# A mixture-of-experts kernel on one core: weight remainders by accumulating DMA, and half 0's way into block 2 a step sooner

## The chip, the cores and the metric

The kernel runs on one core of a Trainium2 chip. The metric is the device time of one execution in microseconds; lower is better. TensorE multiplies, VectorE (DVE), ScalarE (ACT) and GpSimd (POOL) work on arrays, and SyncE (SP) issues transfers. Each engine runs its own instruction stream in order, and semaphores tie the streams together.

## The reference, cut to what matters

Two residual blocks work on 1024 tokens of width 256, in float32. The first picks one of four experts by token id and gates with silu(g) * u where the up and gate weights are the same array; the second picks two of eight experts by a learned router.

```python
x = x + xattn(layernorm(x), token_ids, ctx, ctx, ctx)
#   for e in range(4): y = (silu(h @ W[e].T) * (h @ W[e].T)) @ W[e].T, kept where expert_ids == e
x = x + ffn(layernorm(x), Wg, W1, W2, W3)
#   scores = h @ Wg.T; the best 2 of 8, softmax of their scores as weights w
#   for e in range(8): y += w[e] * (silu(h @ W1[e].T) * (h @ W2[e].T)) @ W3[e].T   (176 hidden units)
```

## The kernel before

Every float32 product is made of three products of rounded operands: an operand is split into a rounded part `hi` (a copy to fp32r) and the remainder `lo` (operand minus `hi`), and hi*hi, hi*lo and lo*hi are summed in PSUM. This holds for the weights (`w_hi`, `w_lo`), the normalised and transposed tokens (`hT_hi`, `hT_lo`) and the activations (`act_hi`, `act_lo`).

The tokens are cut into two halves of 512 columns. The hidden units of all experts together are cut into chunks of 128: 8 in block 1 and 11 in block 2. A step is one chunk of one half in one block, and the 38 steps run in the order block, half, chunk: steps 0 to 7 and 8 to 15 are block 1, 16 to 26 and 27 to 37 are block 2. `up(q)` (L669) writes the step's hidden units into PSUM banks `z` with 6 matmuls of 512 columns in block 1 and 12 in block 2; `down(q)` (L700) adds their product with the down weights into `y[h]` with 12 matmuls of 256 columns. `LAG` is 3: TensorE does `up(q)`, the stages of slot 0, `down(q - 3)`, then the stages of slot 1 (L746 to L759).

Between the two, ScalarE takes silu from PSUM (L416). In block 1 GpSimd multiplies it by the gate (`gated`, L337) and VectorE by the up product (`act`, L587); in block 2 VectorE does both (L577, L587). ScalarE rounds `act` (`round_act`, L388), VectorE takes the remainder (`act_low`, L552). The buffers of these are three deep.

Weights come in 19 pieces, one for each chunk of each block: 8 of 128 x 512 float32 (256 KB) and 11 of 128 x 768 (384 KB). SyncE loads them into a ring of five raw slots (`load_piece`, L249); a slot is loaded again once the remainder of the piece in it is taken (L253). ScalarE makes `w_hi` from a raw piece (`weight_hi`, L350), and the remainder `w_lo` is a subtract on VectorE for the pieces of `VECTOR_LO` ((0,0), (0,5), (0,6), (0,7), L558) and on GpSimd for the other fifteen (L289). `SPLIT_AT` says at which step a piece is split: (0,4) and (0,5) at step 1, (0,6) at 2, (0,7) at 3, then (1,0) at 6, (1,1) at 8, (1,2) at 10, (1,3) at 14 (its subtract on GpSimd a step later, `LATE_LO`), and (1,c) at 12 + c from c = 4 on. `up(q)` waits for the remainder of its piece (`wait_lo`, L671).

Three ways lead tokens into a (block, half) other than the first: into (0,1), (1,0) and (1,1). `STAGES` (L77) gives for each way at what step, counted from `WAY_START` (0, 8 and 16), each engine does its part; for TensorE there is a slot too. A way into block 2 is: the sum of the residual (`add_block`, L501, VectorE), statistics (L460), the power of the variance on GpSimd (L299) and the shift (L306), normalisation of two tiles by VectorE (L485) and two by ScalarE (L371), eight token transposes (L641), `tokens_hi` (L362, ScalarE), `tokens_lo` (L492, VectorE), the router's scores (L653, L657), a copy of them (L433), four score transposes (L665), `best_two` (L507, VectorE), the tanh (L437, ScalarE), the softmax and its gate rows (L527, VectorE), four gate transposes (L627) and the copy `gates_out` (L380, ScalarE). The engines work these in program order within their step: at a step ScalarE does silu, `tokens_hi`, `round_act` of the step before, the score copy, tanh, gates, then the pieces and normalisations due. The first up products of block 2 need `act` of earlier steps: `up(16)` needs act(13) and `up(17)` needs act(15) (L677), since the banks are paired differently; later ones need silu and gated of two steps before (L680). At step 10 VectorE also makes the router's remainder (L594).

## Time and profile before

| | |
|---|---|
| median of 3 runs | 164.11 us (164.03 to 164.11) |
| the profiled execution | 164.04 us |
| its span in the trace | 162.2 us |
| TensorE matmuls busy | 154.5 us, 95% of the span, 904 matmuls |
| VectorE busy | 111.7 us, 69% |
| ScalarE busy | 67.8 us, 42% |
| GpSimd busy | 57.2 us, 35% |
| granted TensorE clock | 0.999 |

The span is the time from the first to the last record of the core; 1.84 us of the execution lie around it. Matmul records overlap, because matmuls are pipelined: one of 512 columns is shown with 0.39 us where the next starts 0.23 us later. So TensorE's pace is read from the starts and not from the durations, and a standstill is a start that comes later than this pace allows. What stands in brackets behind a row of a timeline is the idle time before it and what ended it. The rows are shown below, after the change.

### The profile page before, as it was taken

The page shows a single profiled execution, that of the slowest core. Times are in us where ns is not written, and L with a number is a line of the kernel's source. Part 1 is how long each engine was busy: PE and PEld are TensorE (multiplying, and loading weights), DVE is VectorE, ACT ScalarE, POOL GpSimd, SP SyncE. Part 2 cuts the span into 40 slices and gives each one's busy share as a digit, 9 for nine tenths or more (in the row PEclk, how much of TensorE's full clock was granted, in tenths as well). Part 3 has the DMA queues.
Part 4 walks back from the last instruction along what each step waited for, and adds up shares of the span by engine and source line. Part 5 has one row for each costly group of instructions (what it writes and reads, how often), then busy time and mean ns, then how long its engine had stood idle before and what let it go on. Part 6 is the DMA issues. An engine that isn't in the chain of part 4 may idle for free.

```text
span 162.2 us, 2463 instructions
## 1 busy us (share of the span) xinstructions
PE 154.5 (95%) x904; PEld 131.0 (81%) x904; DVE 111.7 (69%) x224; ACT 67.8 (42%) x121; POOL 57.2 (35%) x50
## 2 busy tenths in 40 slices
PE   7999899899999999999999799999999999999991
PEld 2477698789897788888889488888888888888890
DVE  0878999785986756799999947917444744444453
ACT  3385775754618622474335812324222222222210
POOL 0679956469767480555467310000000000000000
PEclk9999999999999999999999999999999999999999
DMA  3976353032030003033000000000000300000003
GB/s 107 349 246 191 82 203 107 0 97 76 29 97 0 2 0 101 0 97 97 0 4 0 0 0 2 4 0 0 0 0 4 129 0 0 0 2 4 0 0 129
DMA packets 4620, 8.76 MB, mean 54 GB/s; under 512 B 768, under 2 KB 1408, under 8 KB 4608
## 3 DMA queue, kind: packets, MB, share of 16 engines
q1 hardware_dynamic: 4176, 8.34, 16.3%
q10 hardware_dynamic: 432, 0.27, 0.5%
q8 instruction: 7, 0.11, 0.3%
q14 instruction: 5, 0.04, 0.1%
HBM read 7.55 MB, written 1.05 MB: 53 GB/s over the span
## 4 chain that ended last, share of the span: by engine, by line
PE 65%; DVE 21%; issue 4%; ACT 4%; POOL 3%; DVEq 0%; ACTq 0%; POOLq 0%
PE z L685 36%; PE y L710 22%; DVE act L587 5%; PE z L720 4%; DVE act_lo L552 4%; DVE norm L485 2%; DVE w_lo L558 2%; POOL gated L337 2%; DVE stats L468 2%; DVE hT_lo L492 1%; ACT act_hi L388 1%; ACT silu L416 1%; POOL rstd L299 1%; PE y L627 1%; DVE x_sb L498 1%
## 5 line engine op out<-in xcount | busy, mean ns | idle before, releaser
L685 PE MATMUL z<-hT_hi,w_hi 128*128 128x512 f32 x120 | 47.4, 395 | 1.1 <-ACT hT_hi L362 0.9
L685 PE MATMUL z<-hT_hi,w_lo 128*128 128x512 f32 x120 | 47.1, 393 | 0.0
L710 PE MATMUL y<-w_hi,act_lo 128*128 128x256 f32 x152 | 43.5, 286 | 1.0 <-DVE act_lo L552 0.9
L552 DVE TENSOR_TENSOR act_lo<-act,act_hi 128x512 fp32r<-128x512 f32 x38 | 33.6, 884 | 14.8 <-ACT act_hi L388 14.5
L710 PE MATMUL y<-w_hi,act_hi 128*128 128x256 f32 x152 | 43.0, 283 | 0.0
L710 PE MATMUL y<-w_lo,act_hi 128*128 128x256 f32 x152 | 42.9, 283 | 0.0
L416 ACT ACTIVATE silu<-z 128x512 f32<-128x512 f32 x38 | 22.6, 595 | 41.1 <-PE z L685 41.1
L685 PE MATMUL z<-hT_lo,w_hi 128*128 128x512 f32 x120 | 37.3, 392 | 0.0
L289 POOL TENSOR_TENSOR w_lo<-raw,w_hi 128x768 fp32r<-128x768 f32 (+1 forms) x15 | 27.5, 1845 | 20.3 <-ACT w_hi L353 18.9
L388 ACT CAST act_hi<-act 128x512 fp32r<-128x512 f32 x38 | 23.4, 617 | 19.7 <-DVE act L587 19.4
L710 PEld LDWEIGHTS y<-w_hi,act_lo 128*128 128x128 f32 x152 | 29.0, 191 | 3.2 <-DVE act_lo L552 1.5
L577 DVE TENSOR_TENSOR gated<-gate,z 128x512 f32<-128x512 f32 x22 | 15.0, 683 | 22.2 <-PE z L685 20.2
L710 PEld LDWEIGHTS y<-w_lo,act_hi 128*128 128x128 f32 x152 | 29.0, 191 | 1.1
L710 PEld LDWEIGHTS y<-w_hi,act_hi 128*128 128x128 f32 x152 | 29.0, 191 | 0.0
L685 PEld LDWEIGHTS z<-hT_hi,w_hi 128*128 128x128 f32 x120 | 22.7, 189 | 5.3 <-issue 1.6
L685 PEld LDWEIGHTS z<-hT_lo,w_hi 128*128 128x128 f32 x120 | 22.5, 188 | 5.4 <-DVE hT_lo L492 0.5
L685 PEld LDWEIGHTS z<-hT_hi,w_lo 128*128 128x128 f32 x120 | 22.7, 189 | 3.5
L337 POOL TENSOR_TENSOR gated<-silu,gate 128x512 f32<-128x512 f32 x16 | 22.8, 1437 | 7.1 <-ACT silu L416 7.1
L587 DVE TENSOR_TENSOR act<-gated,silu 128x512 f32<-128x512 f32 x22 | 20.0, 908 | 0.0
L353 ACT CAST w_hi<-raw 128x768 fp32r<-128x768 f32 (+1 forms) x19 | 13.9, 743 | 4.1 <-DMA raw<-weights_dram 4.1
L587 DVE TENSOR_TENSOR act<-gated,z 128x512 f32<-128x512 f32 x16 | 10.9, 679 | 1.2 <-POOL gated L337 1.2
L720 PE MATMUL z<-warm_sb 128*128 128x512 bf16 x24 | 7.2, 473 | 1.2 <-DVE warm_sb L561 1.2
(52 smaller groups left out, 80.8 us busy)
## 6 DMA issues: line engine op xcount, KB each, us to landing
raw<-weights_dram SPq DMA_DIRECT2D x11, 384.0 KB, 3.1
raw<-weights_dram SPq DMA_DIRECT2D x8, 256.0 KB, 4.5
x_sb<-x_dram SPq DMA_DIRECT2D x4, 256.0 KB, 4.4
out_dram<-x_sb SPq DMA_DIRECT2D x2, 256.0 KB, 2.5
out_dram<-x_sb SPq DMA_DIRECT2D x2, 128.0 KB, 2.0
out_dram<-x_sb ACTq DMA_DIRECT2D x2, 128.0 KB, 2.1
consts_sb<-consts_dram SPq DMA_DIRECT2D x1, 68.0 KB, 3.7
ids_sb<-token_ids_dram ACTq DMA_DIRECT2D x1, 4.0 KB, 3.9
```

The lines of the kernel that those rows point to most:

```text
L289: nc.gpsimd.tensor_tensor(w_lo[b][:, c, :], raw_piece(b, c), w_hi[b][:, c, :].bitcast(F32), ALU.subtract).then_inc(w_lo_pool, 1)
L337: nc.gpsimd.tensor_tensor(gated[:, q % BUFFERS, :], silu[:, q % BUFFERS, :], gate[:, h, :], ALU.mult)\
L353: nc.scalar.copy(w_hi[b][:, c, :], raw_piece(b, c)).then_inc(w_hi_done, 1)
L388: nc.scalar.copy(act_hi[:, q % BUFFERS, :], act[:, q % BUFFERS, :]).then_inc(act_hi_done, 1)
L416: nc.scalar.activation(silu[:, q % BUFFERS, :], z_banks(q)[0][:], ACT.Silu).then_inc(silu_done, 1)
L468: last = nc.vector.bn_stats(stats[:, t, :], src[:, t, :])
L552: nc.vector.tensor_tensor(act_lo[:, i, :], act[:, i, :], act_hi[:, i, :].bitcast(F32), ALU.subtract)\
L577: nc.vector.tensor_tensor(gated[:, i, :], gate[:, h, :], z_banks(q)[1][:], ALU.mult)\
L587: nc.vector.tensor_tensor(act[:, i, :], gated[:, i, :], factor, ALU.mult).then_inc(act_done, 1)
L685: return nc.tensor.matmul(bank[:], w[b][:, c, cols], tokens[:, h, k, :], **flags)
L710: last = nc.tensor.matmul(o, a[:, q % BUFFERS, rows], w[b][:, c, wd], start=(first and j == 0), stop=(c == CHUNKS[b] - 1 and j == 2), skip ...
L720: nc.tensor.matmul(z[3][:], warm_sb[:, 0:P], warm_sb[:], start=True, stop=True)
```

## The change

Fourteen of the 19 remainders, those of (0,5), (0,6), (0,7) and of all pieces of block 2, are made in another way: ScalarE writes the negated rounded piece into `w_lo` (an activation Copy with scale -1 into fp32r), and then GpSimd issues a DMA that reads the weights from DRAM a second time and adds them onto `w_lo`. `up(q)` waits for that DMA. SyncE may load the raw slot again once the negation is done. VectorE keeps the remainder of (0,0), GpSimd those of (0,1) to (0,4). The late subtract of (1,3) is gone: the DMA is issued at the step of its split. VectorE's three and GpSimd's eleven subtracts are gone; ScalarE has fourteen negations more, each behind the piece's cast, and GpSimd fourteen issues.

Half 0's way into block 2 is one step sooner from the token transposes on (all stages from there to the copy of the gates); its sum, statistics and normalisation stay. The scores of half 1 move at step 23 from slot 0 to slot 1, behind that step's down product.

```diff
-    "transpose_tokens": ((7, 0), (6, 0), (6, 1)),
-    "tokens_hi": (7, 5, 6),
-    "tokens_lo": (6, 4, 6),
-    "scores": (None, (7, 0), (7, 0)),
-    "score_rows": (None, 7, 7),
-    "transpose_scores": (None, (8, 0), (8, 0)),
-    "best_two": (None, 7, 8),
-    "tanh": (None, 7, 8),
-    "softmax": (None, 7, 8),
-    "transpose_gates": ((3, 0), (9, 0), (10, 1)),
-    "gates_out": (2, 8, 9),
+    "transpose_tokens": ((7, 0), (5, 0), (6, 1)),
+    "tokens_hi": (7, 4, 6),
+    "tokens_lo": (6, 3, 6),
+    "scores": (None, (6, 0), (7, 1)),
+    "score_rows": (None, 6, 7),
+    "transpose_scores": (None, (7, 0), (8, 0)),
+    "best_two": (None, 6, 8),
+    "tanh": (None, 6, 8),
+    "softmax": (None, 6, 8),
+    "transpose_gates": ((3, 0), (8, 0), (10, 1)),
+    "gates_out": (2, 7, 9),
...
-VECTOR_LO = ((0, 0), (0, 5), (0, 6), (0, 7))
-LATE_LO = (1, 3)
+VECTOR_LO = ((0, 0),)
+POOL_LO = ((0, 1), (0, 2), (0, 3), (0, 4))
+def by_dma(b, c):
+    return (b, c) not in VECTOR_LO + POOL_LO
...
         def wait_lo(engine, b, c):
-            vector = [p for p in VECTOR_LO if p <= (b, c)]
             if (b, c) in VECTOR_LO:
-                engine.wait_ge(w_lo_vector, len(vector))
+                engine.wait_ge(w_lo_vector, VECTOR_LO.index((b, c)) + 1)
+            elif (b, c) in POOL_LO:
+                engine.wait_ge(w_lo_pool, POOL_LO.index((b, c)) + 1)
             else:
-                engine.wait_ge(w_lo_pool, piece_no(b, c) - len(vector))
+                engine.wait_ge(w_lo_in[b][c], 16)
...
-                    wait_lo(sp, *((0, n) if n < CHUNKS[0] else (1, n - CHUNKS[0])))
+                    last = (0, n) if n < CHUNKS[0] else (1, n - CHUNKS[0])
+                    if by_dma(*last):
+                        sp.wait_ge(w_negated, negated_no(*last))
+                    else:
+                        wait_lo(sp, *last)
...
+            def add_weights(b, c):
+                pool.wait_ge(w_negated, negated_no(b, c))
+                nc.gpsimd.dma_start(w_lo[b][:, c, :], (weights1, weights2)[b][:, c, :], accum_op=ALU.add)\
+                    .then_inc(w_lo_in[b][c], 16)
...
-                if LATE_LO in SPLIT_AT.get(q - 1, ()):
-                    weight_lo(*LATE_LO)
                 for piece in SPLIT_AT.get(q, ()):
-                    if piece not in VECTOR_LO and piece != LATE_LO:
+                    if by_dma(*piece):
+                        add_weights(*piece)
+                    elif piece in POOL_LO:
                         weight_lo(*piece)
...
                 nc.scalar.copy(w_hi[b][:, c, :], raw_piece(b, c)).then_inc(w_hi_done, 1)
+                if by_dma(b, c):
+                    nc.scalar.activation(w_lo[b][:, c, :], raw_piece(b, c), ACT.Copy, scale=-1.0).then_inc(w_negated, 1)
```

## Rows read from the trace of the kernel before

**Rows 1.** The chain of waits in order of time: start us, us, what.
```profile
70.96 2.75 PE z L685 x12
73.71 1.43 PE y L710 x12
```

**Rows 2.** Timeline of TensorE: start us, us, engine, line, operation, tiles, [idle before, releaser].
```profile
19.00 0.63 PE L685 MATMUL z<-hT_lo,w_hi 128*128 128x512 f32 x2
20.22 0.38 PE L710 MATMUL y<-w_hi,act_lo 128*128 128x256 f32 x1 [0.59 <-DVE act_lo L552]
...
30.98 0.28 PE L710 MATMUL y<-w_hi,act_hi 128*128 128x256 f32 x1
31.85 0.47 PE L685 MATMUL z<-hT_hi,w_hi 128*128 128x512 f32 x1 [0.59 <-ACT hT_hi L362]
...
50.33 1.04 PE L641 MATMUL y<-consts_sb,norm 128*128 128x128 f32 x8
51.64 0.39 PE L710 MATMUL y<-w_hi,act_lo 128*128 128x256 f32 x1 [0.27 <-DVE act_lo L552]
...
66.12 0.28 PE L710 MATMUL y<-w_hi,act_hi 128*128 128x256 f32 x1
66.54 0.47 PE L685 MATMUL z<-hT_hi,w_hi 128*128 128x512 f32 x1
...
90.68 0.61 PE L685 MATMUL z<-hT_lo,w_hi 128*128 128x512 f32 x2
92.33 0.62 PE L653 MATMUL y<-hT_hi,router_hl 128*16 128x512 f32 x2 [1.03 <-DVE hT_lo L492]
```

**Rows 3.** Timeline of VectorE, steps 1 to 3, 9 to 11 and 15.
```profile
16.79 1.68 DVE L558 TENSOR_TENSOR w_lo<-raw,w_hi 128x512 fp32r<-128x512 f32 x1
18.39 1.78 DVE L552 TENSOR_TENSOR act_lo<-act,act_hi 128x512 fp32r<-128x512 f32 x1
...
21.79 0.68 DVE L552 TENSOR_TENSOR act_lo<-act,act_hi 128x512 fp32r<-128x512 f32 x1
...
40.70 1.28 DVE L498 TENSOR_TENSOR x_sb<-y,x_sb 128x512 f32<-128x512 f32 x2
...
43.09 1.23 DVE L594 TENSOR_TENSOR router_hl<-router_raw,router_hl 128x16 fp32r<-128x16 f32 x1
44.25 1.39 DVE L468 BATCH_NORM_STATS2 stats<-x_sb 128x6 f32<-128x256 f32 x4
...
46.17 0.16 DVE L476 TENSOR_SCALAR var<-mv 128x4 f32<-128x4 f32 x1
...
60.21 0.19 DVE L512 COPY score_part<-y 128x32 f32<-128x32 f32 x1 [1.22 <-PE y L665]
...
63.09 0.63 DVE L541 COPY gate_rows<-w_tok 128x128 f32<-128x128 f32 x4
```

**Rows 4.** Timeline of ScalarE, steps 1 to 2 and 11.
```profile
15.45 1.14 ACT L353 CAST w_hi<-raw 128x512 fp32r<-128x512 f32 x2
16.50 0.59 ACT L416 ACTIVATE silu<-z 128x512 f32<-128x512 f32 x1
...
48.11 1.09 ACT L371 ACTIVATE norm<-x_sb,shift,rstd 128x256 f32<-128x256 f32 x2 [4.27 <-POOL shift L306]
```

**Rows 5.** Timeline of GpSimd, steps 1 and 11.
```profile
15.38 1.01 POOL L299 TENSOR_TENSOR rstd<-var,minus_half 128x4 f32<-128x4 f32 x1
...
16.62 1.30 POOL L289 TENSOR_TENSOR w_lo<-raw,w_hi 128x512 fp32r<-128x512 f32 x1
...
46.41 1.39 POOL L299 TENSOR_TENSOR rstd<-var,minus_half 128x4 f32<-128x4 f32 x1 [0.86 <-DVE var L476]
```

**Rows 6.** SyncE's timeline, and busy tenths of DMA and issues, 18.6 to 21.5.
```profile
17.94 0.33 SPq L254 DMA_DIRECT2D raw<-weights_dram  x1
...
DMA  0000949413631687999999999998999989999693
...
raw<-weights_dram SPq DMA_DIRECT2D x1, 384.0 KB, 3.5
```

More of the change, by code:

```diff
@@ L187, in ffn_moe @@
         w_in = [[sem(f"w_in{b}_{c}") for c in range(CHUNKS[b])] for b in range(2)]
+        w_lo_in = [[sem(f"w_lo_in{b}_{c}") if by_dma(b, c) else None for c in range(CHUNKS[b])] for b in range(2)]
         w_hi_done, w_lo_pool, w_lo_vector = sem("w_hi_done"), sem("w_lo_pool"), sem("w_lo_vector")
+        w_negated = sem("w_negated")
         router_hi_done, router_lo_done = sem("router_hi_done"), sem("router_lo_done")
@@ L213, in wait_lo, with negated_no @@
         def wait_lo(engine, b, c):
-            vector = [p for p in VECTOR_LO if p <= (b, c)]
             if (b, c) in VECTOR_LO:
-                engine.wait_ge(w_lo_vector, len(vector))
-            else:
-                engine.wait_ge(w_lo_pool, piece_no(b, c) - len(vector))
+                engine.wait_ge(w_lo_vector, VECTOR_LO.index((b, c)) + 1)
+            elif (b, c) in POOL_LO:
+                engine.wait_ge(w_lo_pool, POOL_LO.index((b, c)) + 1)
+            else:
+                engine.wait_ge(w_lo_in[b][c], 16)
+        def negated_no(b, c):
+            return piece_no(b, c) - len(VECTOR_LO) - len(POOL_LO)
         def raw_piece(b, c):
@@ L324, in _ @@
             for c in range(FIRST_PIECES):
-                if (0, c) not in VECTOR_LO:
+                if (0, c) in POOL_LO:
                     weight_lo(0, c)
```

## The prediction

> **What bounds the kernel now.** I read the chain of waits first. From 57 us on it is TensorE nearly without a break: a step of block 2 is 2.75 us of twelve up matmuls and 1.43 us of twelve down matmuls [rows 1]. That is 0.229 us for an up matmul and 0.119 us for a down matmul, so a step of block 1, with six up matmuls, is 1.37 + 1.43 = 2.80 us; nothing in the diff removes or shortens one. So only TensorE's standstills can be won or added. I then read TensorE's timeline for starts that come later than these pitches allow [rows 2]; five of them lie where the diff reaches:
> - before the down product of step 1, 19.00 + 2 x 0.229 = 19.46 against 20.22: 0.76 us, and its first matmul is 0.10 us slower than the pitch. It waits for VectorE's act_lo.
> - before step 8's up product, 30.98 + 0.12 = 31.10 against 31.85: 0.75 us, and 0.16 us in its first matmuls. It waits for ScalarE's hT_hi.
> - after half 0's token transposes (the eight take 1.04 us, of which the next matmul can overlap some 0.14, so 50.33 + 0.90 = 51.23 against 51.64): 0.41 + 0.11 us, act_lo again.
> - before step 18's up product, 66.24 against 66.54: 0.30 + 0.08 us. The gates of half 0 (step 17's transposes) come too late.
> - before half 1's scores, 90.68 + 0.46 = 91.14 against 92.33: 1.19 us, hT_lo.
>
> Sum 0.86 + 0.91 + 0.52 + 0.38 + 1.19 = 3.86 us. That is all that this change can win, whatever it does to the load of the other engines. A shorter busy time of GpSimd or VectorE in block 2 is worth nothing by itself.
>
> **The remainders of pieces (0,5) to (0,7).** VectorE loses three subtracts; the first took 1.68 us at 16.79 and stood ahead of act_lo(1), which then took 1.78 us instead of its free 0.68 us [rows 3]; GpSimd was in its gating pass then. ScalarE gets a negation each, put at its cast's pace, half of 1.14 us [rows 4]. Then act_lo(1) ends near 18.9: ScalarE's two casts end at 16.6, the negation at 17.1, silu(2) and act_hi(1) at some 0.55 us each (the spacing of 0.59 us passes) at 18.2 [rows 4], and act_lo(1) adds 0.68. The down product could start at 19.46, and the 0.86 us go.
>
> What is late next is the new wait. `up(5)` now needs a transfer that has no counterpart in this trace. On GpSimd's queue it stands behind the subtract of piece (0,4), 16.62 + 1.30 = 17.92 [rows 5]; the negation (17.1) is done by then. GpSimd's time to issue it: at least SP's 0.33 us an issue, at most about the 1.39 us that a tiny power takes there [rows 5, 6]. I take 1.0, since both are work done in software rather than an array pass. Data: two plain loads of 384 KB are issued from 17.94 on, and with both in flight the second took 3.5 us; the 16 engines are full from 19.8 to 21.4 [rows 6]. The accumulating 256 KB comes on top. So the landing is bounded by 17.92 + 0.33 + 2.5 = 20.75 (two thirds of that load's 3.5 us) and by 17.92 + 1.39 + twice 3.5 = 26.3 (if reading and adding doubles it). I take 17.92 + 1.0 + 3.5 = 22.4: the load in the same crowd is the nearest row. `up(5)` would otherwise start at 19.46 + 1.43 = 20.9. New standstill: 1.5 + 0.1 us. Queued behind the transfer on GpSimd is gated(2), 18.9 to 20.2 (1.30 us, as the subtract of the same size [rows 5]); act(2) then ends near 20.9, and its down product is due only at 23.8. The transfers of (0,6) and (0,7) are issued behind gated(2) and gated(3), at 20.2 and 22.5, so they would land at 24.7 and 27.0; they are needed at 25.2 and 28.1. They are covered, by 0.5 and 1.1 us.
>
> The Trainium skill (DMA: Bandwidth & Descriptors, Anatomy of one DMA) has a fixed 2.0 us plus bytes over 436 GB/s for a transfer issued from GpSimd. That would be 2.6 us for 256 KB, landing at 20.5, with no standstill at `up(5)`; it is an estimate from the page for a lone plain transfer, and it is what the rival "hidden" below would look like.
>
> **Piece (1,0) and `up(8)`.** `up(4)` ended at 19.46, so it began near 18.0. Without the stall of `up(5)` TensorE's walk 18.0 + 4 x 2.80 + 0.9 + 0.1 gives 30.2 for `up(8)`; with it 31.8. ScalarE now has at step 6 a negation behind the cast of (1,0), half as long again as one of block 1 (768 columns for 512), some 0.8 us, ahead of silu(7) and hT_hi. The other engines' walk: GpSimd has issued (0,7) by 23.5, ScalarE's two normalisations (1.09 us [rows 4]) hold silu(5) to 25.3, gated(5) ends at 26.6, act(5) behind act_lo(4) at 27.4; then ScalarE's act_hi(5) 28.0, cast 28.8, negation 29.5, silu(7) 30.1, hT_hi 30.7. So hT_hi hides behind the down product as long as TensorE is the later one. The 0.91 us go, `up(8)` starts at 31.8, and to there nothing is won: 1.77 us removed, 1.6 added.
>
> **Half 0 one step sooner.** Count from F, the end of the down product of step 7. TensorE reaches the token transposes of step 13 at F + 3 x 1.37 + 2 x 1.43 = F + 7.0 and would end them at F + 7.9. The tokens: sum 1.28, act_lo and act 1.2, the router's remainder (1.23 as measured beside a GpSimd pass, a tenth or two free), statistics 44.25 to 46.33 = 2.08 [rows 3], the power 1.0 to 1.4 and the shift 0.2 (from 16.39 to the subtract's start at 16.62) [rows 5], ScalarE's two normalisations 1.09 [rows 4], and 0.2 for five handovers: F + 7.3 to F + 8.5, and the last 0.55 us of transposes after that. The standstill is between 0 and 1.1 us. I take 0.8 + 0.1, since gated(11) falls on the router's remainder as the subtract did before. It is new, and the 0.52 us behind these transposes goes (the scores of step 14 now stand before that down product).
>
> **Gates of half 0.** From the scores' copy to the last gate row VectorE needs 60.21 to 63.72 = 3.5 us [rows 3]. From the score transposes (step 15) to the gate transposes (step 16, first slot) TensorE has 1.43 + 2.75 = 4.2 us of work. It fits, and the 0.38 us go. But ScalarE now waits for the tanh at step 14, before the cast of (1,3), its negation (0.75 us each) and silu(15); GpSimd has the issue of (1,3) ahead of gated(15). From the copy of the scores: tanh +1.9, cast and negation +3.4, silu +4.0, issue of 1.0 us done by then +4.4, gated(15) 1.3, act(15) 0.7: +6.4. `up(17)` needs act(15) and is due at 4.2 + 0.45 + 1.43 = +6.1. New standstill 0.3 + 0.1 us (none if GpSimd issues in 0.33 us, 0.7 if in 1.4).
>
> **Scores of half 1 behind the down product.** 1.43 us of ready work goes in front of a wait of 1.19 us. It goes wholly; the score copy on ScalarE has the next up product (2.75 us) as cover. VectorE's and ScalarE's passes ahead of hT_lo also get shorter or stay.
>
> **Block 2's other pieces.** (1,4) to (1,10): ScalarE gets 0.74 us a step. Its step is then silu 0.6, act_hi 0.5, cast and negation 1.5, with 1.1 us of normalisations or hT_hi at two steps: 3.7 of 4.18 us. Each transfer has three steps, over 12 us, before its up product. Cost nothing. Loads are released by the negation, earlier or equal.
>
> **The sum.** Removed 3.86; added 1.6 (`up(5)`) + 0.9 (transposes) + 0.4 (`up(17)`) = 2.9. Net -0.96 us: 164.04 - 0.96 = 163.1 us for the profiled run, which is 0.07 under the median 164.11. I predict 163.1.
>
> **Rivals.**
> - Hidden: the transfer lands before 20.9. Then `up(5)` costs nothing, but ScalarE's walk (30.7 against 30.2) becomes the bound at `up(8)` and gives 0.7 back. 163.1 - 1.6 + 0.7 = 162.2. For: loads alone land near 3 us. Against: full DMA engines from 19.8 on [rows 6].
> - The transfer is slow: every 1 us beyond 22.4 is 1 us at `up(5)`. It is slower than before from a landing at 23.4 on; at 24.5 the time is 165.2. For: it reads two places and follows two loads. Against: it is only 256 KB. Later pieces ride behind the same delay, so it is paid once.
> - The earlier way backfires: transposes wait 1.1 and act(15) comes 1 us later than said, because ScalarE and GpSimd wait in turn. 163.1 + 0.3 + 0.9 = 164.3, no change.
> - The change doesn't lighten what it says: GpSimd's issues block it as long as the subtracts (1.3 to 1.8 us). Then issue times above run to the upper ends: 163.1 + 0.4 + 0.3 = 163.8.
>
> **How the numbers follow.** My forecast (162.6 to 163.7) 0.42, hidden (161.6 to 162.6) 0.20, slow transfer 0.20, backfire 0.10, issue as long as subtract 0.08. Some 0.2% (0.33 us) is about what a measurement can tell from no change: faster is below 163.8, slower above 164.4. Faster: 0.42 + 0.20 and a little of the last: 0.63. Same: most of the backfire, half of the last: 0.15. Slower: 0.22. The range leaves out the fast end of "hidden" and the slow end of "slow transfer": 161.8 to 165.2.
>
> **What would show it.** Right: TensorE waits at its fifth up product for a DMA by 1 to 2 us, and the down product of step 1 starts by 19.5; no wait before `up(8)`, before step 18 and before half 1's scores; a wait of 0.5 to 1 us inside the token transposes of step 13; VectorE's passes in block 2 at 0.68 us without the ones over 2 us. Wrong: a landing outside 21.5 to 23.4, waits for (0,6) or (0,7), issues above 1.4 us on GpSimd, or a wait of more than 1 us at `up(17)`.

## The result and the profile after

The changed kernel took 166.91, 167.39 and 168.79 us in three executions (median 167.39), the kernel before 164.11 us beside it (median of four): a ratio of 1.0202, 95% interval [1.0168, 1.0236]. A fourth execution, at 391.25 us, was disturbed and is left out. The change makes the kernel slower, by some 2%, where I had forecast 163.1 us. The profiled execution is the one of 166.91 us, with a span of 165.1 us, 2.9 us more than before.

From the page of the changed kernel (busy us, share of the span, instructions; then DMA queues; then issues with KB each and median us to landing):

```profile
PE 154.5 (94%) x904; PEld 131.2 (79%) x904; DVE 101.9 (62%) x221; ACT 77.4 (47%) x135; POOL 45.6 (28%) x53
...
q0 software_dynamic: 2016, 5.11, 18.8%
q1 hardware_dynamic: 4176, 8.34, 16.2%
...
raw<-weights_dram SPq DMA_DIRECT2D x11, 384.0 KB, 3.6
w_lo<-weights_dram POOLq DMA_DIRECT2D x11, 384.0 KB, 5.4
...
w_lo<-weights_dram POOLq DMA_DIRECT2D x3, 256.0 KB, 6.2
```

TensorE's work is the same 154.5 us. VectorE has 9.8 us less and GpSimd 11.6 us less, ScalarE 9.6 us more. The load did move as intended; the time went the other way. So I repeat the reading of before: where does TensorE stand still? Its timeline after (start us, us, engine, line, operation, tiles, [idle before, releaser]), where lines of `up` are L710 and those of `down` L735:

```profile
19.14 0.62 PE L710 MATMUL z<-hT_lo,w_hi 128*128 128x512 f32 x2
20.97 0.39 PE L735 MATMUL y<-w_hi,act_lo 128*128 128x256 f32 x1 [1.20 <-DVE act_lo L577]
...
22.39 0.28 PE L735 MATMUL y<-w_hi,act_hi 128*128 128x256 f32 x1
24.19 0.50 PE L710 MATMUL z<-hT_hi,w_hi 128*128 128x512 f32 x1 [1.52 <-DMA w_lo<-weights_dram]
...
26.99 0.28 PE L735 MATMUL y<-w_hi,act_hi 128*128 128x256 f32 x1
27.41 0.50 PE L710 MATMUL z<-hT_hi,w_hi 128*128 128x512 f32 x1
...
49.06 0.62 PE L710 MATMUL z<-hT_lo,w_hi 128*128 128x512 f32 x2
50.82 1.55 PE L666 MATMUL y<-consts_sb,norm 128*128 128x128 f32 x8 [1.15 <-DVE norm L510]
52.13 0.36 PE L735 MATMUL y<-w_hi,act_lo 128*128 128x256 f32 x1
...
65.24 0.28 PE L735 MATMUL y<-w_hi,act_hi 128*128 128x256 f32 x1
66.59 0.47 PE L710 MATMUL z<-hT_hi,w_hi 128*128 128x512 f32 x1 [1.07 <-DVE act L612]
```

Taken with the same pitches as [rows 2] (0.229 us for an up matmul, 0.119 for a down matmul), with the slow first matmul behind each gap:

| standstill | before | predicted | after |
|---|---|---|---|
| down product of step 1 (act_lo(1)) | 0.86 | 0 | 1.47 |
| `up(5)` (remainder of (0,5)) | 0 | 1.6 | 1.79 |
| `up(6)` (remainder of (0,6)) | 0 | 0 | 0.40 |
| `up(8)` (hT_hi) | 0.91 | 0 | 0 |
| in and behind half 0's token transposes | 0.52 | 0.9 | 1.79 |
| `up(18)` before, `up(17)` after | 0.38 | 0.4 | 1.30 |
| half 1's scores | 1.19 | 0 | 0 |
| sum | 3.86 | 2.9 | 6.75 |

The sum rises by 2.9 us, and so does the span. Nothing else is needed to account for the profiled run.

The two engines around the first standstill, VectorE's and GpSimd's timelines after:

```profile
16.74 1.29 POOL L306 TENSOR_TENSOR w_lo<-raw,w_hi 128x512 fp32r<-128x512 f32 x1
...
17.98 1.06 POOL L312 DMA_DIRECT2D w_lo<-weights_dram  x1
...
18.26 2.65 DVE L577 TENSOR_TENSOR act_lo<-act,act_hi 128x512 fp32r<-128x512 f32 x1 [1.27 <-ACT act_hi L413]
...
18.80 1.55 POOL L360 TENSOR_TENSOR gated<-silu,gate 128x512 f32<-128x512 f32 x1
...
20.07 1.14 POOL L312 DMA_DIRECT2D w_lo<-weights_dram  x1
...
20.69 1.86 POOL L360 TENSOR_TENSOR gated<-silu,gate 128x512 f32<-128x512 f32 x1
```

VectorE starts act_lo(1) at 18.26, even earlier than the 18.39 of before [rows 3], since its subtract of (0,5) is gone. But it takes 2.65 us where it had taken 1.78 and needs 0.68: it ends 0.56 us behind gated(2), and gated(2) itself comes later, behind the issue.

### The profile page after: what moved, and what is told of

It is laid out like the page before. It is cut to its first block, busy times and chain, and to the rows that moved or that the text cites. A ratio compares the mean times of both kernels' runs of the same rounds, so it can differ in the third digit from the quotient of the medians.

```text
span 165.1 us, 2477 instructions
## 1 busy us (share of the span) xinstructions
PE 154.5 (94%) x904; PEld 131.2 (79%) x904; DVE 101.9 (62%) x221; ACT 77.4 (47%) x135; POOL 45.6 (28%) x53
## 3 DMA queue, kind: packets, MB, share of 16 engines
q0 software_dynamic: 2016, 5.11, 18.8%
## 4 chain that ended last, share of the span: by engine, by line
PE 71%; DVE 8%; POOL 8%; DMA 7%; issue 2%; ACT 2%; DVEq 0%; ACTq 0%; POOLq 0%
PE z L710 41%; PE y L735 27%; DMA w_lo<-weights_dram 4%; POOL w_lo L306 3%; DMA x_sb<-x_dram 2%; POOL gated L360 2%; POOL rstd L322 2%; DVE stats L493 2%; PE y L666 2%; DVE act_lo L577 1%; DVE router_hl L619 1%; DVE act L612 1%; DVE x_sb L643 1%; POOL w_lo L312 1%; PE y L678 1%
## 5 line engine op out<-in xcount | busy, mean ns | idle before, releaser
L710 PE MATMUL z<-hT_hi,w_hi 128*128 128x512 f32 x120 | 47.6, 397 | 3.1 <-DMA w_lo<-weights_dram 1.5
L710 PE MATMUL z<-hT_hi,w_lo 128*128 128x512 f32 x120 | 47.1, 393 | 0.0
L735 PE MATMUL y<-w_hi,act_lo 128*128 128x256 f32 x152 | 43.5, 286 | 1.7 <-DVE act_lo L577 1.7
L735 PE MATMUL y<-w_lo,act_hi 128*128 128x256 f32 x152 | 43.0, 283 | 0.0
L735 PE MATMUL y<-w_hi,act_hi 128*128 128x256 f32 x152 | 43.0, 283 | 0.0
L710 PE MATMUL z<-hT_lo,w_hi 128*128 128x512 f32 x120 | 37.2, 391 | 0.0
L735 PEld LDWEIGHTS y<-w_hi,act_lo 128*128 128x128 f32 x152 | 29.0, 191 | 3.7 <-DVE act_lo L577 1.6
L735 PEld LDWEIGHTS y<-w_lo,act_hi 128*128 128x128 f32 x152 | 29.0, 191 | 1.1
L735 PEld LDWEIGHTS y<-w_hi,act_hi 128*128 128x128 f32 x152 | 29.0, 191 | 0.0
L710 PEld LDWEIGHTS z<-hT_hi,w_hi 128*128 128x128 f32 x120 | 22.7, 189 | 7.7 <-DMA w_lo<-weights_dram 2.1
L413 ACT CAST act_hi<-act 128x512 fp32r<-128x512 f32 x38 | 23.4, 616 | 8.4 <-DVE act L612 8.3
L710 PEld LDWEIGHTS z<-hT_lo,w_hi 128*128 128x128 f32 x120 | 22.5, 188 | 5.2 <-DVE hT_lo L517 0.3
L710 PEld LDWEIGHTS z<-hT_hi,w_lo 128*128 128x128 f32 x120 | 22.7, 189 | 3.6
L312 POOL DMA_DIRECT2D w_lo<-weights_dram x14 | 12.8, 912 | 31.8 <-ACT w_lo L378 31.8
L612 DVE TENSOR_TENSOR act<-gated,silu 128x512 f32<-128x512 f32 x22 | 15.1, 684 | 0.0
L378 ACT ACTIVATE w_lo<-raw 128x768 fp32r<-128x768 f32 (+1 forms) x14 | 11.2, 799 | 0.0
```

Of the source, the lines that this page charges most:

```text
L312: nc.gpsimd.dma_start(w_lo[b][:, c, :], (weights1, weights2)[b][:, c, :], accum_op=ALU.add)\
L378: nc.scalar.activation(w_lo[b][:, c, :], raw_piece(b, c), ACT.Copy, scale=-1.0).then_inc(w_negated, 1)
L413: nc.scalar.copy(act_hi[:, q % BUFFERS, :], act[:, q % BUFFERS, :]).then_inc(act_hi_done, 1)
L612: nc.vector.tensor_tensor(act[:, i, :], gated[:, i, :], factor, ALU.mult).then_inc(act_done, 1)
L710: return nc.tensor.matmul(bank[:], w[b][:, c, cols], tokens[:, h, k, :], **flags)
L735: last = nc.tensor.matmul(o, a[:, q % BUFFERS, rows], w[b][:, c, wd], start=(first and j == 0), stop=(c == CHUNKS[b] - 1 and j == 2), skip ...
```

## The experiments

The first four undo or isolate one part each. What an experiment is compared with is the kernel before, measured beside it (164.1 to 164.4 us); its diff is against the kernel that its text names.

**The remainders by DMA alone.**

```diff
 STAGES = {                # the table of the kernel before, everything else as changed
-    "transpose_tokens": ((7, 0), (5, 0), (6, 1)),
+    "transpose_tokens": ((7, 0), (6, 0), (6, 1)),
...
```

> The changed kernel with the old order of the stages: only the fourteen remainders by DMA. In the changed kernel's trace the standstills at act_lo(1), up(5) and up(6) sum to 3.7 us and replace 1.8 us (before the down product of step 1 and before step 8). Theory A (the remainders carry the loss): some 2 us slower than before, so 166.0. Theory B (the stages moved sooner carry it): within 0.3 us of before, 164.1.

Measured: 166.37 us, ratio 1.0104 [1.0069, 1.0140]. Theory A holds. Its ten times fall in two groups, four of 164.99 to 165.22 and six of 166.3 to 166.98. The mean granted clock of TensorE is 0.996 to 1.0 in the first group and 0.985 to 0.99 in the second. That scatter, which the kernel before doesn't have, became a question of its own.

**The moved stages alone.**

```diff
 STAGES = {                # the table of the changed kernel, everything else as before
-    "transpose_tokens": ((7, 0), (6, 0), (6, 1)),
+    "transpose_tokens": ((7, 0), (5, 0), (6, 1)),
...
```

> The kernel before with all stages moved as in the change, remainders as before. It wins 1.2 us at half 1's scores. At half 0 it trades 0.9 us of standstills (before the down product of step 11, before step 18) for a wait in the token transposes of step 13 and one before up(17). Theory A: those two new waits come from the stages' own chain (statistics, power, tanh ahead of silu(15)) and are as long as in the changed kernel, 1.8 and 1.3 us: 164.1 - 1.2 - 0.9 + 3.1 = 165.1. Theory C: the negation and the issue ahead of silu(15) and gated(15) make the second wait; without them it is nearly gone: 163.8.

Measured: 165.48 us, ratio 1.0070 [1.0052, 1.0087]. The token transposes wait 1.35 us (I had expected 1.8) and `up(17)` 1.37 us, without any DMA remainder. Theory A holds and C falls: the negation and the issue aren't needed for the second wait. So half 0's earlier way loses as it stands, and hides the gain at half 1's scores.

**Half 1's scores alone.**

```diff
-    "scores": (None, (7, 0), (7, 0)),
+    "scores": (None, (7, 0), (7, 1)),
```

> The kernel before with only half 1's scores moved behind the down product of step 23. Every theory: the standstill of 1.19 us goes and nothing replaces it, 164.1 - 1.2 = 162.9.

Measured: 163.01 us, ratio 0.9917 [0.9890, 0.9944]. As expected; this part alone beats the kernel before.

**Block 1's remainders back on VectorE.**

```diff
-VECTOR_LO = ((0, 0),)
+VECTOR_LO = ((0, 0), (0, 5), (0, 6), (0, 7))     # all else as in the changed kernel
```

> The changed kernel with the remainders of (0,5), (0,6), (0,7) on VectorE again; all eleven of block 2 stay with the DMA. Theory A (the loss sits in block 1's three transfers, their landing of over 6 us and GpSimd's issue holding act_lo back): the standstills to step 8 fall from 3.7 us to the 1.8 us of before or less, so about 2 us under the changed kernel, 165.2. Rival (the transfers of block 2 hurt too, by the memory or the port): it stays above 166.5.

Measured: 164.68 us, ratio 1.0007 [0.9990, 1.0024]. The loss by DMA sits in block 1's three transfers. A new thing showed: `up(8)` waits 1.49 us for hT_hi. ScalarE's timeline of this run:

```profile
29.90 0.62 ACT L413 CAST act_hi<-act 128x512 fp32r<-128x512 f32 x1 [2.62 <-DVE act L612]
30.42 0.83 ACT L376 CAST w_hi<-raw 128x768 fp32r<-128x768 f32 x1
...
31.16 0.84 ACT L378 ACTIVATE w_lo<-raw 128x768 fp32r<-128x768 f32 x1
31.91 0.57 ACT L441 ACTIVATE silu<-z 128x512 f32<-128x512 f32 x1
...
32.38 1.06 ACT L387 CAST hT_hi<-y 128x512 fp32r<-128x512 f32 x2
```

The negation of (1,0) (0.75 us to the next pass) stands ahead of hT_hi as the prediction said. It costs its full length here, 1.49 us of waiting against 0.75 before. In the changed kernel it costs nothing, only because TensorE is late there.

**The moved stages, repaired in two places.**

```diff
-ROUTER_STEP = 10
+ROUTER_STEP = 7           # in the kernel of the moved stages alone
```

> The stages moved as in the change, remainders as before, and the router's remainder at step 7 instead of 10, off the chain between half 0's sum and its statistics. Its pass took 1.23 us there (beside GpSimd's subtract). Theory A (that chain sets the wait in the token transposes of step 13): the wait falls from 1.35 us by up to 1.2 us, and the time by about as much against the stages alone, 165.5 to 164.4. Rival (the wait hangs on the power on GpSimd or on ScalarE): it stays at 1.3 us and so does the time.

Measured: 164.54 us, ratio 1.0017 [0.9998, 1.0035]: 0.9 us under the stages alone. The wait in and behind the transposes fell from 1.35 to 0.68 us in the profile. A pass of 1.23 us on 16 columns [rows 3], which takes 0.67 us where no GpSimd pass lies beside it, was on the chain.

```diff
 ROUTER_STEP = 7
-SPLIT_AT |= {q: ((1, c),) for c, q in enumerate((6, 8, 10, 14))}
+SPLIT_AT |= {q: ((1, c),) for c, q in enumerate((6, 8, 10, 15))}
```

> The same, and piece (1,3) is split at step 15 (its subtract at 16) instead of 14. Theory A (up(17) waits since the cast of (1,3) stands ahead of silu(15) and its subtract on GpSimd holds act_lo(14) and so act(15)): the 1.37 us before up(17) go, and with the scores' 1.2 us the kernel reaches about 162.6, under the kernel with the scores alone. Rival (act(15) is late because of the tanh and nothing else): the wait shrinks by the cast's 0.7 us at most, 163.7.

Measured: 163.09 us, ratio 0.9916 [0.9886, 0.9946], and no wait at `up(17)` is left. VectorE and GpSimd around act(15), first with the split at 14 (the stages alone), then at 15:

```profile
60.28 1.29 POOL L337 TENSOR_TENSOR gated<-silu,gate 128x512 f32<-128x512 f32 x1 [4.94 <-ACT silu L416]
...
61.53 1.85 POOL L289 TENSOR_TENSOR w_lo<-raw,w_hi 128x768 fp32r<-128x768 f32 x1
61.58 2.35 DVE L552 TENSOR_TENSOR act_lo<-act,act_hi 128x512 fp32r<-128x512 f32 x1
...
63.85 0.67 DVE L587 TENSOR_TENSOR act<-gated,z 128x512 f32<-128x512 f32 x1
```

```profile
59.05 1.30 POOL L337 TENSOR_TENSOR gated<-silu,gate 128x512 f32<-128x512 f32 x1 [4.21 <-ACT silu L416]
60.98 0.69 DVE L552 TENSOR_TENSOR act_lo<-act,act_hi 128x512 fp32r<-128x512 f32 x1
...
61.58 0.68 DVE L587 TENSOR_TENSOR act<-gated,z 128x512 f32<-128x512 f32 x1
```

The subtract that began 0.05 us before act_lo(14) held it for its whole length, and act(15) stands behind act_lo(14). The edit also takes the cast of (1,3) from ahead of silu(15), so gated(15) comes sooner as well; the two shares aren't separated. The rival (the tanh alone) would have left a wait. But 163.09 us is no better than the scores alone: repaired, half 0's earlier way is about worth what the later one was.

**What makes the landing late: the addition or the crowd.**

```diff
-                nc.gpsimd.dma_start(w_lo[b][:, c, :], (weights1, weights2)[b][:, c, :], accum_op=ALU.add)\
+                nc.gpsimd.dma_start(w_lo[b][:, c, :], (weights1, weights2)[b][:, c, :])\
```

The rest is the changed kernel.

> The changed kernel with the fourteen transfers as plain ones from GpSimd, without the addition (w_lo is then overwritten with the weights instead of becoming the remainder; the addition is left out). Landings in the changed kernel: 4.7 to 7.3 us from the start of the issue, 6.2 for (0,5). Theory D (adding onto the destination makes the transfers slow): landings fall to about an issue of 0.9 us plus the 3.1 to 3.6 us of plain loads, 4.0 to 4.5, and up(5) waits at most 0.3 us; 1.5 us or more under the changed kernel. Theory E (the way through GpSimd or the crowd of loads makes them slow): landings stay at 5 to 7 us and up(5) waits 1.5 us.

Measured: 164.92 us, ratio 1.0038 [1.0015, 1.0061]. All fourteen landings went from 4.7 / 5.9 / 7.3 us (least, median, most, from the start of the issue) to 3.2 / 4.1 / 5.4, that of (0,5) from 6.2 to 4.7, and `up(5)` waited 0.51 us. The addition costs a transfer 1.5 to 1.9 us; of this the issue on GpSimd is some 0.3 us (0.53 to 0.78 us plain, 0.86 to 1.14 with the addition). The same 2016 packets and 5.11 MB took 10.3% of the DMA engines' span plain and 18.8% with the addition. Theory D is right on the direction but not all of it: `up(5)` still waited. And not all of the gain is at `up(5)`. With the shorter issues act_lo(1) took 2.46 us instead of 2.65, and the wait before `up(17)` was 0.92 us instead of 1.23.

The other half of the question, in the kernel with the remainders by DMA alone:

```diff
             def load_piece(b, c):
+                if (b, c) == (1, 1):
+                    for k in (5, 6, 7):
+                        sp.wait_ge(w_lo_in[0][k], 16)
```

> The kernel with the remainders by DMA and the old stages; SyncE holds the plain loads of (1,1) and later back until (0,5), (0,6), (0,7) have landed. Theory I (the crowd of two 384 KB loads makes (0,5) land 6.2 us after the start of its issue): it lands after 4.3 to 4.8 us like the fastest of block 2, so near 22.5; up(5) waits some 0.2 us instead of 1.8, as act_lo(1) still holds the down product to 20.9. About 1.5 us under the 166.4: 164.9. Rival (the addition alone takes the 6 us): it lands at 24 as before, 166.4.

Measured: 163.75, 163.78, 166.70 and 166.82 us. In the profiled execution (163.78 us) (0,5) landed 4.1 us after the start of its issue with the addition still in it, where the same kernel without this edit has 6.3, and `up(5)` doesn't wait. So the crowd of two plain loads of 384 KB costs some 2 us. Both theories hold, one half each; no run takes both away at once. The issues of (0,5) as the three kernels' DMA views list them (the changed kernel; plain; loads later):

```profile
w_lo<-weights_dram POOLq DMA_DIRECT2D x1, 256.0 KB, 6.2
```

```profile
w_lo<-weights_dram POOLq DMA_DIRECT2D x1, 256.0 KB, 4.7
```

```profile
w_lo<-weights_dram POOLq DMA_DIRECT2D x1, 256.0 KB, 4.1
```

**What holds act_lo(1).** First, does GpSimd's issue itself hold a pass of VectorE that reads two arrays in SBUF? The changed kernel gets plain transfers more:

```diff
+                if 29 <= q < 34:
+                    pool.wait_ge(gated_done, q + 1)
+                    for k in range(3):
+                        nc.gpsimd.dma_start(raw[:, q - 29, k * D:(k + 1) * D], weights2[:, q - 29, k * D:(k + 1) * D])...
```

> The changed kernel with 15 plain transfers of 128 KB more, issued by GpSimd three by three in steps 29 to 33, behind VectorE's gated, so that they lie beside act_lo and act, both of which read two arrays in SBUF; nothing else runs on GpSimd there. Theory P (GpSimd's issue holds VectorE's two-array passes as its array passes do): those of the passes that begin inside an issue take 1.0 to 3 us instead of 0.68. Theory Q (only GpSimd's array passes hold them; in the changed kernel it was gated behind the issue): all stay at 0.68 to 0.70 us.

```profile
125.36 1.66 POOL L374 DMA_DIRECT2D raw<-weights_dram  x3 [27.46 <-DVE gated L609]
125.51 0.69 DVE L584 TENSOR_TENSOR act_lo<-act,act_hi 128x512 fp32r<-128x512 f32 x1 [0.45 <-ACT act_hi L420]
126.11 0.68 DVE L619 TENSOR_TENSOR act<-gated,silu 128x512 f32<-128x512 f32 x1
```

No: both passes lie inside the issues and keep 0.68 us, in the other steps too. Theory Q. The same execution (168.69 us) happened to show act_lo(1) at 4.95 us:

```profile
18.43 4.95 DVE L584 TENSOR_TENSOR act_lo<-act,act_hi 128x512 fp32r<-128x512 f32 x1 [1.27 <-ACT act_hi L420]
...
19.10 1.55 POOL L361 TENSOR_TENSOR gated<-silu,gate 128x512 f32<-128x512 f32 x1
...
20.96 1.86 POOL L361 TENSOR_TENSOR gated<-silu,gate 128x512 f32<-128x512 f32 x1
```

It ends 0.56 us behind gated(3): it waited for gated(2), and then for gated(3) too. TensorE stood still for 3.57 us ahead of that down product, and then ran at the lower of its two clock levels, 1.2 GHz, for 3.4 us (stretch, length, busy us of each engine, granted clock, share and rate of the DMA engines):

```profile
23.40:26.80 3.40, 3.36 (x14) 3.27 (x15) 1.97 (x4) 2.79 (x6) 0.82 (x2) 0.50 0.89 221
```

So the price of such an execution has three parts: 2.2 us more of waiting at act_lo(1) (3.57 against 1.37), some 1.4 us by the clock (the down product and `up(5)` took 4.43 us together instead of 3.0), and 1.8 us back, since `up(5)` no longer has to wait for (0,5). The sum, 1.8 us, is an estimate from these rows; this execution took 1.8 us more than the profiled one of the changed kernel. The mean granted clock is 0.99 here, as in the execution of 168.79 us of the changed kernel.

Then, does an accumulating issue hold it? In the kernel with the remainders by DMA alone:

```diff
                     if by_dma(*piece):
+                        if b == 1:
+                            pool.wait_ge(gated_done, q + 1)
                         add_weights(*piece)
```

> The same kernel, the transfers of (1,4) to (1,10) issued only once VectorE's gated of the step is done, so that an accumulating issue of 0.88 us of 384 KB stands beside act_lo or act, which read two arrays in SBUF. The 128 KB plain issues left these at 0.69 us. Theory G (an accumulating issue is no different): 0.68 to 0.70 us again, and act_lo(1)'s first wait has another reason. Theory H (it holds VectorE's two-array passes for its length): passes that begin inside an issue take up to 1.5 us.

Measured (165.48 us, one execution): an accumulating issue of 0.86 us at 73.47 had act_lo beside it at 73.60 with 0.69 us and act at 74.21 with 0.68 us. Theory G: an accumulating issue doesn't hold them either. Next, in the same base kernel, the three issues of block 1 behind the gating pass of the next step:

```diff
+                for piece in SPLIT_AT.get(q - 1, ()):
+                    if by_dma(*piece) and piece[0] == 0:
+                        add_weights(*piece)
                 for piece in SPLIT_AT.get(q, ()):
-                    if by_dma(*piece):
+                    if by_dma(*piece) and piece[0] == 1:
                         add_weights(*piece)
```

> The kernel with the remainders by DMA and the old stages, but GpSimd issues the transfers of (0,5), (0,6), (0,7) one step later, behind gated(2), gated(3), gated(4). Theory F (at act_lo(1) the issue and then gated hold VectorE one behind the other): act_lo(1) takes 1.8 us as before instead of 2.67, the down product of step 1 starts at 20.2 instead of 20.9, gated(3) can't overtake it, and the runs scatter less than the 165.0 to 167.0 of before this edit. The landing of (0,5) comes 1.3 us later, though, so up(5) waits until some 25.5; the time is 1 us or more above the 166.4. Rival (the issue's place is of no matter to VectorE): act_lo(1) stays at 2.6 us.

Measured: 169.33 us, ratio 1.0290 [1.0244, 1.0336]. act_lo(1) takes 1.58 us and the down product starts at 19.82, a little better than expected; but (0,5) is issued at 19.17, lands 7.6 us later, and `up(5)` waits 5.42 us. Here too the clock fell in the long standstill, and stayed low behind it:

```profile
25.00:31.60 6.60, 4.83 (x16) 4.26 (x17) 1.43 (x4) 1.10 (x2) 1.18 (x1) 0.50 0.57 126
```

From 26.77 to 31.94 `up(5)` and the down product behind it took 5.17 us where the pitches give 2.80. So some 2.3 us of this kernel's loss are the clock. The order on GpSimd matters to VectorE as theory F has it, and the later landing, with the clock behind it, costs more than that.

Does gated(3) make the upper group? The base of the next two is the kernel with the remainders by DMA alone and its loads held back:

```diff
                 if b == 0:
+                    if q == 3:
+                        pool.wait_ge(act_lo_done, 2)
                     pool.wait_ge(silu_done, q + 1)
```

> The kernel with remainders by DMA, old stages and the plain loads held back (its runs fell on 163.75 or 166.8), and GpSimd waits for act_lo(1) ahead of gated(3). Theory J (in the slow runs gated(3) gets ahead of the waiting act_lo(1), which then takes 4.9 us instead of 2.7): no run is above 164.5 any more, all near 163.8. Rival (the slow runs come from the landings): runs near 166.8 remain.

Measured: 164.11 us, ten runs from 163.78 to 164.54, where the kernel without this wait had two of four above 166.6 (granted clock 0.99). Theory J: the longer executions are those in which gated(3) too gets ahead of the waiting act_lo(1). That rests on the counts (two of four against none of ten) and on the one trace above; no execution of the upper group of this kernel was traced.

> The same with the wait ahead of gated(2) in place of gated(3). Theory K (gated(2) alone holds act_lo(1), from its start on, though act_lo(1) begins 0.5 us before it): act_lo(1) takes 0.69 us at 18.2, the down product of step 1 starts at 19.5, and 1.4 us go there; up(5) may get back some 0.7 to 1.4 us of it, since (0,5) lands at 22.0 and the product is then due at 20.9: 163.0 to 163.7. Theory H (the issue of (0,5) holds it): act_lo(1) takes 1.5 us, to the issue's end at 19.0 plus its own 0.68.

The same edit with `q == 2`. Measured: 163.63 us, ratio 0.9967 [0.9947, 0.9987]. Its timeline:

```profile
17.78 1.05 POOL L315 DMA_DIRECT2D w_lo<-weights_dram  x1
18.05 0.69 DVE L581 TENSOR_TENSOR act_lo<-act,act_hi 128x512 fp32r<-128x512 f32 x1 [1.27 <-ACT act_hi L417]
18.83 1.34 POOL L364 TENSOR_TENSOR gated<-silu,gate 128x512 f32<-128x512 f32 x1
```

act_lo(1) takes 0.69 us inside the issue. gated(2) is recorded 0.1 us later than in the base kernel (18.72) and ends at 20.17 instead of 20.29. Theory K, and H falls. The wait that remains is at `up(5)`: 1.49 us, since its turn now comes at 20.8.

**Do the causes account for all?**

In the kernel with the wait ahead of gated(2):

```diff
-    "scores": (None, (7, 0), (7, 0)),
+    "scores": (None, (7, 0), (7, 1)),
```

> The one with the wait ahead of gated(2), and half 1's scores behind the down product of step 23. If the causes add, its time is that of the one above less 1.2 us: 161.8 to 162.5, and the remainders by DMA are then as good as the subtracts (162.9 to 163.0 with the scores alone) or a little better.

Measured: 163.68 us, ratio 0.9954 [0.9935, 0.9973], the same as without the scores' move. My expectation failed: the causes don't add here. In the kernel without the move the scores follow the up product with no gap:

```profile
91.46 0.61 PE L714 MATMUL z<-hT_lo,w_hi 128*128 128x512 f32 x2
91.92 0.63 PE L682 MATMUL y<-hT_hi,router_hl 128*16 128x512 f32 x2
```

The remainders by DMA had already taken the 1.19 us away. In the kernel before, VectorE was a step behind there, with four passes held beside GpSimd's subtracts: an act_lo of 2.14 us, two normalisations of 2.26, and the `act` of step 21:

```profile
87.28 2.32 DVE L587 TENSOR_TENSOR act<-gated,silu 128x512 f32<-128x512 f32 x1
86.97 2.08 POOL L289 TENSOR_TENSOR w_lo<-raw,w_hi 128x768 fp32r<-128x768 f32 x1 [0.96 <-ACT w_hi L353]
```

Without the subtracts that `act` takes 0.68 us, and hT_lo comes in time.

The change with four repairs (the diff is shortened to one line each):

```diff
-ROUTER_STEP = 10                                             +ROUTER_STEP = 7
-enumerate((6, 8, 10, 14))                                    +enumerate((6, 8, 10, 15))
+                if (b, c) == (1, 1):                         # SyncE: wait for w_lo_in of (0,5), (0,6), (0,7)
+                    if q == 2:                               # GpSimd: pool.wait_ge(act_lo_done, 2)
```

> The change as it is, with four repairs: plain loads from (1,1) on held back until block 1's three transfers have landed, GpSimd waiting for act_lo(1) ahead of gated(2), the router's remainder at step 7, and (1,3) split at step 15. If the loss lies in these four places and nowhere else, the standstills of 1.5 + 1.8 + 0.4 (block 1), 1.7 (token transposes, to some 0.7) and 1.3 (up(17)) go but for 1 us at up(5) and perhaps 0.7 at up(8) behind the negation of (1,0): 167.0 - 4.5 = 162.5, below the kernel before. Rival (something else in the change costs): 164 or more.

Measured: 162.63 us, ratio 0.9897 [0.9868, 0.9927]: ten runs, eight of 162.26 to 163.48 and two at 164.4 and 164.8. As expected, and some 4.8 us under the change's 167.39. It has the lowest median of the study; its lead over half 1's scores alone (163.01 us, ratio 0.9917) is less than what the two intervals can tell apart. In its profile (163.48 us) `up(5)` still waits 1.19 us and `up(8)` 0.55 us. The four repairs were tried together here; how much each is worth in this kernel isn't shown.

**A version without DMA remainders.** The stages with both repairs, and piece (1,0) split behind hT_hi:

```diff
-SPLIT_AT |= {q: ((1, c),) for c, q in enumerate((6, 8, 10, 15))}
+SPLIT_AT |= {q: ((1, c),) for c, q in enumerate((7, 8, 10, 15))}
```

> No DMA remainders: stages as in the change, the router's remainder at step 7, (1,3) split at step 15, and (1,0) split at step 7 instead of 6, behind hT_hi on ScalarE. ScalarE's cast of (1,0) stands ahead of silu(7) and hT_hi, and up(8) waits 0.75 us with 0.16 us of slow first matmuls. If the cast sets that wait, it goes by 0.7 us: 163.1 - 0.8 = 162.3, the fastest kernel so far. Rival (GpSimd's subtract of (1,0), now a step later, holds VectorE's remainders of hT or act and gives it back): 163.1.

Measured: 162.99 us, ratio 0.9931 [0.9911, 0.9950], the same as without this edit. The wait of 0.75 us before `up(8)` did go, but the wait ahead of the token transposes was 0.82 us again, not 0.27. The gain was given back later. The traces show where: TensorE reached the transposes 0.88 us sooner (end of the up product before them), the sum of half 0 on VectorE only 0.32 us (40.66 against 40.98). That sum stands behind act(9), which waited 1.18 and 1.19 us for GpSimd's gated(9) in the two kernels, and GpSimd was busy without a break from 32.79 to 41.28, with both subtracts and the gating passes of three steps. The router's remainder did lie beside the subtract of (1,0) (1.23 us instead of 0.67), but VectorE stood idle for 1.19 us one pass later, so this cost nothing there. It is a reading of two traces; no run moves GpSimd's passes away.

## Why the prediction was wrong

Three terms of its sum failed: the wait for act_lo(1), put at 0, measured 1.47 us; the wait at half 0's token transposes, put at 0.9, measured 1.79; and the wait at `up(17)`, put at 0.4, measured 1.30. Behind the first and the third, and in part behind the second, is the same step: the prediction left out a two-array pass of VectorE, or priced it too short, where a pass of GpSimd would lie beside it. Point by point:

- **What bounds the kernel.** Right: TensorE's work didn't change, and the standstills sum to the whole difference. Wrong was the sentence that less load on VectorE in block 2 is worth nothing. It was worth the 1.19 us before half 1's scores, as gated2_waits and dma_repaired_scores show; the moved scores were worth the same 1.19 us, and only one of the two could have it.
- **act_lo(1), predicted 0, measured 1.47 us.** The largest miss. I gave act_lo its free 0.68 us since VectorE's subtract was gone. What had made it 1.78 us before was GpSimd's gating pass, which I named and then left out. The change doesn't take that pass away; it puts an issue ahead of it, so that it ends at 20.35, where before it was out of act_lo(1)'s way by 19.5. gated2_waits gives the 0.69 us that I had assumed.
- **`up(5)`, predicted 1.6, measured 1.79 us.** The size is near by luck: two errors cancel. The landing was 24.2 and not 22.4, inside my bounds (20.75 to 26.3), but the product's turn came at 22.5 instead of 20.9, because of act_lo(1). Issue 1.06 us (predicted 1.0), data 5.1 us (predicted 3.5). Left out one at a time, the addition was worth 1.5 us of the landing and the crowd 2 us. I had priced the crowd and not the addition. That the price is one for one at `up(5)` was right; so was the rival "the transfer is slow" as a mechanism. It wasn't the cause of the result alone.
- **(0,6), predicted covered, measured 0.40 us.** It landed 7.3 us after its issue at 20.07, where I had taken 4.5.
- **`up(8)`.** Right: no wait, as TensorE is late. With block 1's pieces on VectorE the negation costs 0.74 us there (1.49 against 0.75), near the 0.7 of the rival "hidden", so the walk of ScalarE was right as well.
- **Half 0 a step sooner, predicted 0.9, measured 1.79 us.** From the end of step 7's down product (42.49 by the starts) to the end of the last normalisation (51.55) it took 9.1 us. My bounds were 7.3 to 8.5, of which I took a value near 8.2; the terms as listed add up to 8.7 at the upper end, so the bound itself was 0.2 too low. The router's remainder took 1.57 us beside gated(11), the power 1.41, both at or above the top of what I had allowed. The down product behind the transposes waits for the last of these normalisations and for nothing else: its act_lo(10) was done at 49.27. stages_router7 shows the router's share: 0.7 us of the wait.

```profile
45.03 1.59 POOL L360 TENSOR_TENSOR gated<-silu,gate 128x512 f32<-128x512 f32 x1
45.09 1.57 DVE L619 TENSOR_TENSOR router_hl<-router_raw,router_hl 128x16 fp32r<-128x16 f32 x1
...
50.46 1.09 ACT L396 ACTIVATE norm<-x_sb,shift,rstd 128x256 f32<-128x256 f32 x2 [4.64 <-POOL shift L329]
```

- **`up(17)`, predicted 0.4, measured 1.30 us.** The chain was right to 0.3 us up to gated(15). I had left out act_lo(14), which stands ahead of act(15) on VectorE. gated(15) (63.67 to 65.29, behind the issue at 63.03) held it for 2.09 us, as gated(2) held act_lo(1), and act(15) began at 65.77, half a us behind the end of gated(15). The stages alone waited as long (1.37 us) with another GpSimd pass, the subtract of (1,3), on act_lo(14).

```profile
63.67 1.62 POOL L360 TENSOR_TENSOR gated<-silu,gate 128x512 f32<-128x512 f32 x1
63.75 2.09 DVE L577 TENSOR_TENSOR act_lo<-act,act_hi 128x512 fp32r<-128x512 f32 x1 [0.92 <-ACT act_hi L413]
...
65.77 0.68 DVE L612 TENSOR_TENSOR act<-gated,z 128x512 f32<-128x512 f32 x1
```

- **The rival "backfires"** named the right two places, priced them at 1.2 us above my forecast and gave them one chance in ten.

The Trainium skill (SBUF — State Buffer, Who interferes with whom) says that a VectorE pass with two inputs in SBUF contends with a GpSimd pass that reads SBUF, and that the order of issue decides who blocks. The first rule is borne out wherever act_lo takes 1.6 to 5 us here instead of 0.69. On the second the records differ: act_lo(1) is recorded from 18.26, gated(2) from 18.80, and act_lo(1) still waited for it, but not once gated(2) had to wait for act_lo(1). Starts on GpSimd are rough, though: gated(2) is recorded 0.24 us before the issue ahead of it ends (17.98 + 1.06). The Trainium skill (SBUF — State Buffer, Who interferes with whom) also has it, as inferred, that writing a transfer's descriptors needs the write side, while such a VectorE pass takes only the read side; issue_beside and add_beside agree (0.68 to 0.69 us).

The Trainium skill's 2.0 us plus bytes over 436 GB/s (DMA: Bandwidth & Descriptors, Anatomy of one DMA) would be, as estimates, 2.3 us for 128 KB, 2.6 for 256 and 2.9 for 384. From the start of the issue the plain 128 KB transfers of issue_beside, with little else in flight, landed after 2.3 to 2.5 us, which agrees, and the fastest plain one of 384 KB in plain_dma after 3.2. With the addition no 256 KB transfer landed in under 3.9 us, and (0,5), with two loads beside it, took 6.2; for these the measurement decides.

What stays open: how GpSimd's pass gets ahead of a VectorE pass that the trace shows as begun 0.5 us earlier, what decides between the 2.65 and the 4.95 us, and what makes two of ten runs of the changed kernel with four repairs 2 us longer. Their granted clock is 0.99, as after the long standstills above, but neither was traced. Its profiled run has 1.18 us before the first down product, behind act_lo(0). The trace shows the start of that: two small VectorE passes on 4 columns, the last of half 1's statistics in block 1, took 1.01 and 1.33 us beside gated(0) and gated(1), where they took 0.40 and 0.15 in the changed kernel. Not every execution has it.

## What to carry to other kernels

Count a pass on a shared port by what runs on the other engine at that moment: moving or delaying a pass of GpSimd can cost VectorE more than removing one saves, and a single wait that orders the two is a cheap repair (here it gave act_lo(1) back 2 us and cost GpSimd 0.1, though only 0.5 us reached the kernel's time, 163.63 against 164.11 with the wait a step later, because `up(5)` then waited for its transfer). When two parts of a change remove the same standstill, only one of them earns it; sum over standstills, not over parts. A transfer that replaces an engine pass close to its use must be priced with the traffic that is in flight then (2 us here), and one that adds onto its destination with some 1.5 us more. A standstill of TensorE can cost more than its length: with 3.57 and 5.42 us of it came 3.4 and some 6.7 us at half the clock.

## What the runs showed of the hardware

- GpSimd's issue of a transfer of 128 rows took 0.86 to 1.14 us with the addition (changed kernel), 0.53 to 0.78 us plain (plain_dma), and 1.6 us for three plain ones of 128 KB in a row; VectorE's two-array passes beside it kept 0.68 to 0.69 us.
- An accumulating transfer landed 4.7 to 7.3 us after the start of its issue in the changed kernel, a plain one in its place 3.2 to 5.4 us; the same bytes kept the DMA engines busy for 18.8% of the span instead of 10.3%.
- A VectorE pass of 0.68 us that reads two arrays in SBUF can be passed over by two GpSimd passes in a row (4.95 us). The times of two kernels with this place fall in two groups, 1.6 and 3 us apart, and one wait on GpSimd removes the upper one (163.78 to 164.54 in ten runs).
- TensorE stood still for 3.57 us in issue_beside and ran at a granted clock of 0.50 from 23.4 to 26.8; in issue_behind_gated it was 5.42 us, and 0.50 from 25.0 to 31.6. In the profiled run of the changed kernel, with standstills of 1.37 and 1.68 us, the granted clock was 1.00 from 18 to 32 us.
